# A four-layer graph network in one program: half-tile norms for batches 0 and 1, one sum over nodes instead of two, a mask in one VectorE operation

## The reference

```
x = layernorm(x + adj @ (x @ W0) + b0)                                   # layer 0
# layer 1: res[i,j] = x_i.wi + x_j.wj + adj[i,j]*wr + gb
x = layernorm(x + (res @ x) @ W1 + b1)
# layer 2: h = elu(x @ Wi + bi); e = sigmoid(at_i + as_j + be) * mask
# mask = adj + ALPHA * (adj == 0), ALPHA = 0.005
# out = concat(elu(concat(e @ h, h * rowsum(e)) @ Wn + bn), h) @ Wm + bm
x = layernorm(x + out)
# layer 3: five steps of a gated unit, m = adj @ h in each
h = x; repeat 5: z, r = sigmoid(...m, h...); v = tanh(...m, r*h...); h = (1-z)*h + z*v
x = layernorm(x + h)
```

## Time and profile before

| | |
|---|---|
| three executions | 1234.6, 1237.77, 1240.07 us |
| profiled execution, its own time | 1235.95 us |
| its span in the trace | 1234.0 us |
| TensorE busy | 1172.3 us, 95% |
| VectorE busy | 927.5 us, 75% |
| ScalarE busy | 684.7 us, 55% |
| mean granted TensorE clock | 0.988 |

### The profile page before, as it was taken

How to read it: one execution, slowest core, us unless ns; L and a number is a source line. 1 busy time by engine, 2 the same in 40 slices (tenths; PEclk the granted TensorE clock), 3 DMA queues, 4 the chain that set the end, 5 groups by cost and what they waited for, 6 DMA issues and landing times.

```text
span 1234.0 us, 15530 instructions
## 1 busy us (share of the span) xinstructions
PE 1172.3 (95%) x5232; PEld 907.4 (74%) x5232; DVE 927.5 (75%) x2071; ACT 684.7 (55%) x1119; POOL 74.5 (6%) x80
## 2 busy tenths in 40 slices
PE   7979899799999999999999999999999999999995
PEld 5866368577777878877777677887777768788884
DVE  5987986588878886677887886685798788554656
ACT  4336762666566675356567565546457657544443
POOL 0110010000000011001000001000001002000001
PEclk9999999899999999999999999999999999999997
DMA  7222330132222322121232322211332322000001
GB/s 249 87 76 94 102 112 1 34 120 78 94 94 85 95 86 88 41 77 60 92 96 78 128 94 69 69 52 52 104 111 86 111 78 86 18 1 1 1 1 35
DMA packets 92575, 93.66 MB, mean 76 GB/s; under 512 B 9104, under 2 KB 62992, under 8 KB 92496
## 3 DMA queue, kind: packets, MB, share of 16 engines
q1 hardware_dynamic: 92352, 92.27, 23.0%
q0 software_dynamic: 144, 0.40, 0.1%
HBM read 65.35 MB, written 27.29 MB: 75 GB/s over the span
## 4 chain that ended last, share of the span: by engine, by line
PE 58%; DVE 22%; ACT 6%; issue 4%; DMA 4%; SPq 4%; POOL 2%; DVEq 0%; POOLq 0%; ACTq 0%
PE ps L813 33%; PE ps L818 4%; PE ps L820 4%; PE ps L819 4%; PE ps L936 4%; DVE ring L1544 3%; PE ps L831 3%; ACT x L1133 3%; DMA mk<-mask_scratch 2%; SPq L693 2%; DVE tl L1359 2%; DVE hT L1598 1%; DVE v L1595 1%; PE ps L824 1%; DVE ml L1359 1%
## 5 line engine op out<-in xcount | busy, mean ns | idle before, releaser
L813 PE MATMUL ps<-adj_hi,xh 128*128 128x512 f32 x672 | 281.6, 419 | 13.1 <-DVE xl L1359 7.1
L813 PE MATMUL ps<-adj_hi,xl 128*128 128x512 f32 x672 | 263.0, 391 | 0.0
L813 PE MATMUL ps<-adj_lo,xh 128*128 128x512 f32 x672 | 262.5, 391 | 0.0
L813 PEld LDWEIGHTS ps<-adj_hi,xh 128*128 128x128 f32 x672 | 126.7, 189 | 50.4 <-issue 19.0
L813 PEld LDWEIGHTS ps<-adj_lo,xh 128*128 128x128 f32 x672 | 126.8, 189 | 32.6 <-issue 8.9
L813 PEld LDWEIGHTS ps<-adj_hi,xl 128*128 128x128 f32 x672 | 126.4, 188 | 27.3
L1577 DVE TENSOR_TENSOR r<-r,hT 128x512 f32<-128x512 f32 x80 | 53.7, 688 | 76.8 <-ACT r L1271 76.8
L818 PE MATMUL ps<-mh,wh 128*128 128x512 f32 x240 | 101.9, 425 | 6.7 <-DVE ml L1359 5.2
L1544 DVE TENSOR_TENSOR ring<-ring,mk 128x512 f32<-128x512 f32 x128 | 86.9, 685 | 27.2 <-ACT ring L1206 23.9
L1206 ACT ACTIVATE ring<-fh,asn 128x512 f32<-128x512 f32 x96 | 67.3, 719 | 62.6 <-DVE mk L1359 21.5
L1128 ACT ACTIVATE mh<-ps 128x512 fp32r<-128x512 f32 x80 | 47.2, 590 | 92.0 <-PE ps L813 92.0
(11 more groups left out here) (295 smaller groups left out, 2374.2 us busy)
## 6 DMA issues: line engine op xcount, KB each, us to landing
mk<-mask_scratch SPq DMA_DIRECT2D x128, 256.0 KB, 2.8
state_scratch<-v SPq DMA_DIRECT2D x60, 256.0 KB, 2.0
tl<-state_scratch SPq DMA_DIRECT2D x192, 64.0 KB, 2.0
x<-in_x SPq DMA_DIRECT2D x8, 512.0 KB, 4.1
out<-x SPq DMA_DIRECT2D x7, 512.0 KB, 3.2
...
```

What stands on the lines that cost most here:

```text
L813: mm = pe.matmul(dst, a[:, t, :], b[:, t, cut(h)], start=(t == 0 and i == 0), stop=(t == T - 1 and i == 2))
```

## The change

Five edits, and new tables for all engines.

1. Batches 0 and 1: `v`, `n` and `l` are done by halves of four tiles (`v0a v0b`, `n0a n0b`, `l1a l1b`, and so on), each with its own statistics, moments, `pow` and scalings. `m1` of these batches may start when the first half of the low part is there, and waits for the second at tile 4.
2. The start of layer 3 for batches 0 and 1 is part of `n2a n2b` (ScalarE) and of new pieces `l2a l2b` (VectorE); it stands in the tables, no longer at the end of the `first` list and of unit 0.
3. Layer 1: x tiles are 129 columns wide, the last one constant 1. `sums` multiplies x^T by [x, 1] (128x129 for 128x2), so the row dots with wj (eight per batch) are gone; the constant row is now a per-partition bias of ScalarE's copy of `m1`, which also scales by wr. `rows` needs one matmul and one broadcast instead of two each; `kb` is gone. `sums` moves ahead of `m1` in the chain of its PSUM bank.
4. `mask`: ScalarE scales the block by 1/ALPHA, VectorE does `(a == 0) + a` in one operation; two weight matrices are scaled by ALPHA on ScalarE (in `weights`).
5. All tables are new.

```diff
+HALVED = (0, 1)
-        xs = [bufs(f"x{q}_", [P, T, D]) for q in range(2)]
+        xs = [bufs(f"x{q}_", [P, T, D + 1]) for q in range(2)]
...
                 elif name == "sums":
-                    seen(pe, "sj", b)
+                    for h in range(2):
+                        seen(pe, half("xn0", h, b), b)
                     bank = bank_free(name, b)
                     for t in range(T):
-                        mm = pe.matmul(ps[:, bank, 0:2], x[:, t, :], f["sv"][:, t, 0:2],
+                        mm = pe.matmul(ps[:, bank, 0:D + 1], x[:, t, :], x_wide(b)[:, t, :],
                                        start=(t == 0), stop=(t == T - 1))
...
                 elif name == "rows":
-                    for i in range(2):
-                        mm = pe.matmul(ps[:, bank, tile(i)], f["bc"][:, i, :], w1f[:, :], start=True, stop=True)
-                    tell(mm, "rw", b)
+                    tell(pe.matmul(ps[:, bank, 0:D], f["bc"][:, :], w1f[:, :], start=True, stop=True), "rw", b)
...
             def state_product(s, h, p, i, prev, breaks):
-                if i == 0:
-                    pe.wait_ge(n_xl[s], p + 1)
+                if i == 0 and p == 0:
+                    seen(pe, "xl3a", s)
+                elif i == 0:
+                    pe.wait_ge(n_xl[s], p)
...
                 if name == "mask":
+                    act.wait_ge(s_al, b + 1)
+                    act.activation(stage[b], stage[b], ACT.Copy, scale=1.0 / ALPHA).then_inc(s_scaled, 1)
                     return
                 if name == "weights":
                     act.wait_ge(s_comb, 1)
                     copy(wh[:, :, :], mkflat[:, 0:5, :]).then_inc(s_wh, 1)
+                    act.wait_ge(s_w, 16 * W_LOADS)
+                    for weight in (wx[:, 0:D], wf[:, WNB, :]):
+                        act.activation(weight, weight, ACT.Copy, scale=ALPHA).then_inc(s_wh, 1)
                     return
...
                     if name[1] == "1":
                         seen(act, "sj", b)
-                    tell(copy(f["m"][:, cut(h)], ps[:, BANKS_A[b][h], :]), "mc" + name[1:], b)
+                        seen(act, "k", b)
+                        ins = act.activation(f["m"][:, cut(h)], made, ACT.Identity, bias=f["sc"][:, 1:2], scale=wr)
...
+                    elif name in ("n2a", "n2b"):
+                        seen(act, "xn" + name[1:], b)
+                        tell(copy(xh[b][:, at, :], x[:, at, :]), "xh3" + name[2], b)
...
-                dve.tensor_scalar(noedge, stage[t], 0.0, ALPHA, ALU.is_equal, ALU.mult).then_inc(s_noedge, 1)
-                dve.wait_ge(s_noedge, n + 1)
-                dve.tensor_tensor(stage[t], stage[t], noedge, ALU.add).then_inc(s_mask, 1)
+                dve.wait_ge(s_scaled, n + 1)
+                dve.scalar_tensor_tensor(out=stage[t], in0=stage[t], scalar=0.0, in1=stage[t],
+                                         op0=ALU.is_equal, op1=ALU.add).then_inc(s_mask, 1)
...
                 elif name == "d1":
-                    seen(dve, "xn0", b)
-                    tell(row_dots(f["m"], x, wjb, lambda t: f["sv"][:, t, 1:2]), "sja", b)
-                    seen(dve, "sja", b)
-                    tell(row_dots(f["m"], x, wib, lambda t: f["sv"][:, t, 2:3]), "sj", b)
+                    tell(row_dots(f["m"], x, wib, lambda t: f["sv"][:, t:t + 1]), "sj", b)
...
                 elif name == "sums":
+                    tell(dve.tensor_tensor_reduce(out=f["bc"][:, :], in0=ps[:, bank, 0:D], in1=wjb, scale=1.0,
+                                                  scalar=0.0, op0=ALU.mult, op1=ALU.add, accum_out=sc[:, 1:2]),
+                         "sja", b)
...
-                if not prev:
-                    start_natural(1, p)
```

More of the change, by code:

```diff
@@ L76 @@
     "PE": """
[L77 to L81, removed]
@@ L91 @@
-unit8 @4 e07:3 @5 rva:3 @11 y2a:3 e10:3 @17 e11:3 @18 e12:3 @21 e13:3
-unit9 @4 e14:3 @10 e15:3 @16 e16:3 rsb:3 e17:3 @17 rvb:3 @22 y2b:3
-unit10 @21 m0a:4 @26 m0b:4
-unit11 @1 y0a:4 @3 y0b:4 @22 m1a:4 @24 m1b:4 @26 sums:4
+first m0a:0 m0b:0 y0a:0 y0b:0 m0a:1 m0b:1 y0a:1 sums:0 m1a:0 m1b:0 y0b:1 m0a:2 rows:0 y1a:0 sums:1 y1b:0
+first m1a:1 m1b:1 t2a:0 m0b:2 rows:1 t2b:0 pja:0 pjb:0 y1a:1 y1b:1 y0a:2 y0b:2 tha:0 thb:0 tga:0 tgb:0 t2a:1
+first e00:0 e01:0 e02:0 t2b:1 e03:0 pja:1 e04:0 e05:0 e06:0 sums:2 m1a:2 pjb:1 e07:0 m1b:2 e10:0 e11:0 e12:0
@@ new lines @@
+first rsa:0 e13:0 e14:0 tha:1 e15:0 rows:2 rva:0 e16:0 e17:0 thb:1 y1a:2 y1b:2 tga:1 tgb:1 y2a:0 rsb:0 e00:1
+first e01:1 e02:1 rvb:0 e03:1 e04:1 e05:1 m0a:3 e06:1 e07:1 y2b:0 m0b:3 e10:1 e11:1 e12:1 y0a:3
+unit0 @2 e13:1 e14:1 e15:1 y0b:3 e16:1 e17:1 @4 rsa:1 @7 rsb:1 @8 pja:2 rva:1 sums:3 m1a:3 rvb:1 m1b:3 y2a:1 rows:3 y1a:3 y2b:1 pjb:2 y1b:3 @19 th0:2 th1:2 @22 th2:2
+unit1 @22 e00:2 e01:2 e02:2
+unit2 @12 e03:2 @21 e04:2 e05:2 @22 e06:2 @26 rsa:2
+unit3 @2 e07:2 @3 rva:2 @8 e10:2 @9 y2a:2 e11:2 @22 e12:2 e13:2 @24 e14:2
@@ L97 @@
-unit14 @3 th2:4 @11 m1a:5 @18 m1b:5 e00:4 sums:5 e01:4 e02:4 e03:4 @21 e04:4 e05:4 rows:5 @22 e06:4
-unit15 @8 e07:4 y1a:5 rsa:4 @12 e10:4 e11:4 e12:4 rva:4 @22 y1b:5 e13:4
-unit16 @2 e14:4 y2a:4 e15:4 e16:4 @10 e17:4 rsb:4 @15 rvb:4 @22 y2b:4
+unit13 @21 m0a:5 @23 m0b:5 pja:4 pjb:4 y0a:5 @25 y0b:5 @27 th0:4 th1:4
+unit14 @10 th2:4 sums:5 @18 m1a:5 @21 m1b:5 e00:4 e01:4 @24 rows:5 e02:4
+unit15 @11 e03:4 @16 e04:4 e05:4 y1a:5 e06:4 rsa:4 e07:4 y1b:5 @22 e10:4 @25 e11:4 e12:4
+unit16 @1 e13:4 e14:4 e15:4 rva:4 @6 e16:4 @7 e17:4 @9 y2a:4 @11 rsb:4 @16 rvb:4 @22 y2b:4
@@ L106 @@
-unit23 @21 m0a:7 @23 m0b:7 pja:6 y0a:7 pjb:6 @24 y0b:7 @27 th0:6
-unit24 @6 th1:6 @10 th2:6 @11 m1a:7 @19 m1b:7 @22 e00:6 e01:6
-unit25 @1 e02:6 sums:7 e03:6 e04:6 @3 e05:6 @5 e06:6 e07:6 @11 rsa:6 rows:7 @17 e10:6 e11:6 @22 y1a:7 e12:6 rva:6 e13:6 @25 e14:6 @27 y2a:6
-unit26 @4 e15:6 @6 y1b:7 e16:6 @10 rsb:6 @12 e17:6 @16 rvb:6 @22 y2b:6
-unit27 @13 pja:7 @14 pjb:7 @21 th0:7 th1:7 @23 th2:7
+unit21 @1 y0a:6 @6 y0b:6 @22 sums:6 m1a:6
+unit22 @9 m1b:6 @11 rows:6 @18 y1a:6 @21 y1b:6
+unit23 @19 m0a:7 @22 m0b:7 pja:6 y0a:7 pjb:6 @23 y0b:7 @26 th0:6 th1:6
@@ L208 @@
+unit29 @1 rva:7 s13:7 @4 s14:7 s15:7 s16:7 s17:7 y2a:7 @5 rsb:7 rvb:7 @11 y2b:7 @15 v2:7
 unit30
```

333 lines of the change are left out of this document (178 added, 155 removed).

## The result

The changed kernel took **1244.59 us** (median of 7 executions, 1242.21 to 1245.25) against 1237.77 us before (now 7 executions, with the same median and the same ends). The ratio is **1.0055, with a 95% interval of 1.0041 to 1.0069**: 6.8 us slower. Forecast were 1227 us, a range of 1217 to 1236 and a chance of 0.04 for slower. The prediction was wrong in sign.

The account below looks back on a forecast made before the run. The prediction took a chain over three engines to bound the stage before unit 1, and TensorE the body. Terms 8.5 - 8.9 - 1.6 - 8.8 + 2.0 - 0.3 = -9.1 from 1235.95 gave 1227 us, range 1217 to 1236.

Parts of the forecast that it names:

- front of the tables: Before batch 1's first product: the new order makes TensorE wait for batch 1's low part, +8.5 us with slow clock.
- edit 2: hole, slow clock, new wait: At unit 1's start: hole -7.1 us and slow clock -1.75 us go; a new wait in unit 1 costs +2.0.
- wait for `ml` in unit 0: TensorE's wait in unit 0 behind ScalarE's scalings and copy `mh` goes with the norm earlier: -1.6 us.
- VectorE's relief: row dots and masks: Before unit 1: VectorE loses row dots (-6.8 us) and one mask operation of two (-5.8 us), all on the path.
- VectorE's other terms: Before unit 1: `kb` -1.2 us, second broadcasts -0.8, new reductions +1.2, moment operations done twice +4.5.
- TensorE's matmuls: In eight batches: `rows` loses a matmul, -2.1 us; `sums` gets wider, +1.8 us; net -0.3 us.
- rival (e): At the front: x loads slow down from the 516-byte stride and weights land 2.9 us later, 1230 us; chance 0.06.
- rival (b): Before unit 1: VectorE's relief falls beside the path and its 8.9 us become idle time, 1236 us; chance 0.15.
- rival (c): Unit 1 waits again, for the split or DMA targets, some 5 us instead of 2, 1230 us; chance 0.10.
- ScalarE's masks: Eight mask operations of about 1 us beside TensorE's first products, counted at nothing; 1 us if the cover were gone.
- Rival (d): Around the first attention tiles: `m1a` comes later, so TensorE only follows VectorE's tiles, 1243 us; chance 0.04.

Follow-up runs that it names:

- a_xlast: The changed kernel with its 129-column x tiles allocated behind all others, so `xh` and later tiles lie where they lay before: 0.9982 of the kernel before.
- b_late: The kernel before with the changed order at the front: batch 1's product behind both `y0` of batch 0, batch 1's low part behind the weights: 1.0063.
- b_nat4: b_nat3 with the load `k03` of batch 2 moved on SyncE from its first list into unit 1: 0.9949 of the kernel before.
- a_both: a_xlast with the wj row dots done again for nothing and the mask made in two VectorE operations without ScalarE: 1.0006 of the kernel before.
- a_early: a_xlast with batch 1's first half product (TensorE) and low part (VectorE) back at their old places at the front: 0.9944 of the kernel before.
- b_nat: The kernel before with only layer 3's start for batch 1 moved directly behind unit 0's second `m` split: 1.0004 of the kernel before.
- b_nat3: b_nat with the changed kernel's tables in units 1 to 5, batch 2's fourth attention tile moved to unit 2: 0.9999 of the kernel before.

## Why the prediction was wrong

The parts, each as measured by its own runs, against its term (the forecast of -8.9 for VectorE is split into the parts that were put back and the rest):

| part | forecast | measured | by |
|---|---|---|---|
| place of `xh` against `adj` | not seen | +9.0 | after / a_xlast |
| front of the tables | +8.5 | +7.8 | b_late |
| edit 2: hole, slow clock, new wait | -8.8 + 2.0 = -6.8 | -6.3 | b_nat4 |
| wait for `ml` in unit 0 | -1.6 | -1.3 | traces: 1.59 before, 0.26 after |
| VectorE's relief: row dots and masks | -12.6 | -3.0 | a_both |
| VectorE's other terms | +3.7 | not separated | |
| TensorE's matmuls | -0.3 | not separated | |
| sum | -9.1 | +6.2 | the change itself: +6.8 |

The measured terms are good to about 2 us each and come from different kernels, so that their sum falls this near to 6.8 is partly luck.

- **The step that was missing**: the prediction goes through the edits one after another and nowhere asks what else moves when x tiles become 129 columns wide. The only thing I followed from the wider tile was rival (e), the loads; they got no slower. The combined weights' first operation starts at 25.02 us instead of 25.41. The Trainium skill ("DMA: Bandwidth & Descriptors", "How a descriptor splits into AXI transactions") would have three transactions for two there, by the prediction's estimate 0.4 us in all; two single executions can't show so little in either direction. What 128 bytes did to the products is 9.0 of the 15.9 us between forecast and result; with it cured the kernel is at 0.9982 (0.9970 to 0.9994), 2.2 us below before.
- **The step that failed** is "I take all, since VectorE is full in 92% of the earlier trace rows's middle row, and it is there that TensorE waited for it". That row is of 120 to 180 us. In the changed kernel VectorE is 9.1 us less busy in it and TensorE's idle time falls from 6.0 to 5.4 us. All masks and half of the row dots lie before 84 us, where TensorE was idle for 2.7 of 54 us before: whatever is taken off VectorE there, no more than that could be won while TensorE's work stays. The forecast itself had just put "eight half products" in a row on TensorE, with `rows` behind them at 84, said that VectorE has to wait for them, and then took VectorE's relief off the path all the same; the 12.8 us of waiting for `rows` are where it went. This is rival (b), which I gave 0.15, and its 1236 us is what a_xlast shows (0.9982 of 1237.77 is 1235.5). The relief was taken at the far end of its range; 12.6 us of it measured 3.0 behind the late front, and the whole of it 0.9 us at unit 1 with the old front (a_early against b_nat4).
- **Edit 2** was right in kind and in size. That nothing else would be late right behind it was wrong for the kernel before (b_nat to b_nat3). The forecast of 2.0 us for a new wait priced VectorE's splits, where the neighbours in line were the targets, which rival (c) did name, and the queue of SyncE, which nobody named. The changed tables had provided for all of them.
- **The front** was right in every number: batch 1's product at 30.07 (30 to 31), clock 0.50 behind it, `rows` of batch 1 at 84.52 (83 to 85), the first tile at 100.70 (below 103). Unit 1 at 219 to 223 was missed: 230.57, and 228.97 with the tiles back in place. From `rows` on, the forecast needed the relief to be won as well as the hole, and only the hole was.
- **ScalarE's masks** priced at nothing: nothing speaks against it. In the changed kernel TensorE is busy without a gap beside them, and with the old front the waits for ScalarE are 2.3 us with them and 2.05 without.
- **Rival (d)** named the sign and came near the time, 1243, by another road: that is luck. One half of its condition was met (VectorE idle for 17.0 us between 70 and 125, more than 8), the other wasn't: between 90 and 120 us TensorE is idle for 6.9 us and not 12.
